# A four-sequence decoder on one core: queries and keys of the attention as two twelve-bit float32r parts in half-array operands, instead of three bf16 parts over the whole array

## The reference, cut to what matters

```python
# WINDOW
scores = jnp.einsum('bnqhd,bnkhd->bnhqk', qp, kp) * scale
attn = jax.nn.softmax(scores, axis=-1)
out = jnp.einsum('bnhqk,bnkhd->bnqhd', attn, vp).reshape(B, L, D)
...
scores = jnp.einsum('bqhd,bkhd->bhqk', q, k) / jnp.sqrt(jnp.asarray(hd, h.dtype))
causal = jnp.tril(jnp.ones((S, S), bool))
scores = jnp.where(causal, scores, jnp.asarray(-1000000000.0, h.dtype))
a = jax.nn.softmax(scores, axis=-1)
out = jnp.einsum('bhqk,bkhd->bqhd', a, v).reshape(B, S, D)
```

## Time and profile before

| what | value |
|---|---|
| three runs | 1493.69, 1497.62 and 1497.46 us; median 1497.46 us |
| profiled execution, span of core 0 | 1493.0 us (the page gives no other time of it) |
| TensorE busy | 1369.8 us, 92% |
| VectorE busy | 1085.1 us, 73% |
| ScalarE busy | 795.1 us, 53% |
| mean DMA rate | 106 GB/s |

### The profile page before, as it was taken

How to read it: one execution, slowest core, us unless ns; L and a number is a source line. 1 busy time by engine, 2 the same in 40 slices (tenths; PEclk the granted TensorE clock), 3 DMA queues, 4 the chain that set the end, 5 groups by cost and what they waited for, 6 DMA issues and landing times. The chain is left out here.

```text
span 1493.0 us, 29555 instructions
## 1 busy us (share of the span) xinstructions
PE 1369.8 (92%) x9483; PEld 763.5 (51%) x9519; DVE 1085.1 (73%) x2623; ACT 795.1 (53%) x1507; POOL 156.6 (10%) x185
## 2 busy tenths in 40 slices
PE   6878989999999999999999999999999989889990
PEld 3556566664454544443353343343545445578990
DVE  5786744457664777789999999998868877563325
ACT  5375755536647666665455465555666545323332
POOL 1101011100100100001010000000000003224223
PEclk8799999999999999999999999999999989999996
DMA  6223323301402542434343333122222231676754
GB/s 230 79 68 102 104 48 86 86 26 27 127 23 80 163 122 52 137 94 121 104 143 98 93 123 86 51 65 53 62 53 56 52 105 57 206 292 194 213 182 179
DMA packets 124482, 158.32 MB, mean 106 GB/s; under 512 B 31372, under 2 KB 103820, under 8 KB 122348
## 3 DMA queue, kind: packets, MB, share of 16 engines
q1 hardware_dynamic: 120930, 147.06, 33.9%
q0 software_dynamic: 3408, 9.38, 1.7%
HBM read 66.38 MB, written 29.44 MB: 64 GB/s over the span
## 5 line engine op out<-in xcount | busy, mean ns | idle before, releaser
L1668 ACT ACTIVATE prob<-ps 128x512 f32<-128x512 f32 (+3 forms) x832 | 404.0, 550 | 202.8 <-PE ps L1441 108.1
L1960 DVE TENSOR_REDUCE mx<-ps 128x1 f32<-128x512 f32 (+3 forms) x512 | 281.3, 585 | 80.3 <-PE ps L1409 42.4
L1441 PE MATMUL ps<-of_expert 99*128 99x512 bf16 (+4 forms) x768 | 252.4, 357 | 8.2 <-DMA of_expert<-mrow 3.3
L1441 PEld LDWEIGHTS ps<-of_expert 99*128 99x128 bf16 (+1 forms) x768 | 73.1, 98 | 95.5 <-ACT prob L1668 35.7
L1476 PE MATMUL ps<-prob,va 128*32 128x512 f32 (+3 forms) x1024 | 117.0, 530 | 0.2
L1407 PE MATMUL ps<-of_expert 120*128 120x512 bf16 x256 | 92.0, 380 | 3.6 <-DVE mx L1960 0.4
L1401 PE MATMUL ps<-of_expert 96*128 96x512 bf16 x256 | 86.7, 381 | 6.2 <-DVE mx L1956 5.3
L1956 DVE CUSTOM_DVE_ANT_0 ps<-ps,room_a 128x512 f32<-128x512 f32 x128 | 86.1, 710 | 5.5 <-PE ps L1401 5.2
L1956 DVE CUSTOM_DVE_ANT_0 ps<-ps,room_b 128x512 f32<-128x512 f32 x128 | 85.9, 708 | 1.7 <-PE ps L1401 1.4
L1398 PE MATMUL ps<-of_expert 96*128 96x128 bf16 (+3 forms) x256 | 72.4, 306 | 9.0 <-DVE mx L1960 7.3
L1658 ACT ACTIVATE mrow<-ps 12x512 bf16<-12x512 bf16 x64 | 37.2, 581 | 77.3 <-PE ps L1423 77.2
(11 more groups left out here) (251 smaller groups left out, 2550.4 us busy)
## 6 DMA issues: line engine op xcount, KB each, us to landing
of_expert<-parts SPq DMA_DIRECT2D x384, 128.0 KB, 2.4
sorted<-zeros SPq DMA_DIRECT2D x27, 650.0 KB, 7.7
room_a<-in_w SPq DMA_DIRECT2D x30, 512.0 KB, 4.1
otc<-oraw SPq DMA_DIRECT2D x256, 32.0 KB, 2.0
room_b<-in_w SPq DMA_DIRECT2D x15, 512.0 KB, 4.2
ct<-in_c SPq DMA_DIRECT2D x8, 512.0 KB, 3.8
of_expert<-in_w SPq DMA_DIRECT2D x8, 512.0 KB, 8.2
wa<-in_attention SPq DMA_DIRECT2D x4, 768.0 KB, 5.0
```

Source lines behind the costliest of these rows:

```text
L1441: i = pe.matmul(dst[:, lo:S], ks[0:rows, h, t], qs[0:rows, h, lo:S], start=(a != MASKED), stop=(a != CAUSAL and not fixed))
L1668: act.activation(prob[:, quad % PROBS, n, lo:S], key_bank(*st)[:, lo:S], ACT.Exp).then_inc(s_exp, 1)
L1960: i = dve.tensor_reduce(mx[:, slot, s, n:n + 1], src[:, 0:width], AX.X, ALU.max)
```

## The change

- A projected query or key is split into two parts instead of three: ACT writes the first as `float32r` (`F32R`), DVE subtracts and writes the second as `float32r`. The step SL is gone, with L1648 and L1933.
- An operand row set of a head is 64 rows instead of 96 to 126: three slots of 16 rows with parts (first by first, first by second, second by first), and a fourth slot for extra rows: two for the maximum, fourteen for the ALiBi lines. Even heads lie in partitions 0 to 63 and odd heads in 64 to 127 (`place_of`), so a score matmul takes up one half of the array's rows. The operands have a tile of their own, `operands`, in float32.
- The scores S and T multiply `float32r` by `float32r`. Corrections, triangles and masks stay bf16 or float16 matmuls over all 128 rows.
- P has two DVE steps instead of four. M transposes 8 columns of float32 instead of 12 of bf16.
- OP issues three DMAs of parts of 256 KB instead of six of 128 KB, and for queries one more that refills the fourth slot from a DRAM scratch (`extra_rows`). At the start a GpSimd DMA casts all extra rows from the input into that scratch, and the keys' extra rows are loaded once, at the end of the first loads.
- The planner's costs follow. TensorE is modelled as two halves (`turn_of_array`): a score matmul waits for its own half, everything else for both. `SWITCH` is added to a correction, triangle or mask. The `LAG` table is another one, so the order of all engines is new.

```diff
+F32R = mybir.dt.float32r
-Q_PARTS = (0, 0, 1, 1, 0, 2)
-K_PARTS = (0, 1, 0, 1, 2, 0)
-ROWS = len(Q_PARTS) * HD
...
+Q_PARTS = (0, 0, 1)
+K_PARTS = (0, 1, 0)
+SLOTS = len(Q_PARTS) + 1
+EXTRA = SLOTS - 1
+HALF = P // 2
...
+def place_of(h):
+
+    return HALF * (h % 2), h // 2
...
-        pe = 0.23
+        pe, after = 0.22, 0.0
+        if a == WINDOW:
+            pe = 0.3
         if a == ALIBI:
-            pe += sum(0.004 + 0.00042 * max(60, hi - lo) for _, lo, hi, _ in corrections(J * g + n, s))
+            after = sum(0.004 + 0.00042 * max(60, hi - lo) for _, lo, hi, _ in corrections(J * g + n, s))
+            after += SWITCH if after else 0.0
         if a == CAUSAL:
-            pe = 0.055 * (s + 2)
+            pe, after = 0.055 * (s + 1), 0.06 + SWITCH
+        pe = (0.0, pe, after, n % 2)
...
+SWITCH = 0.05
...
-LAG = {"IN": -3.7, "CA": 26.5, ("CA", 1): 25.9, "FS": 13.8, "OP": -5.3, ("OP", 0): 1.6, ("OP", 1): -4.0, ("OP", 3): 2.1, "M":
+LAG = {"IN": 12.1, "ZF": -62.0, "EI": 5.1, ("EI", 0): -5.2, ("EI", 1): -6.3, ("EI", 2): 4.6, "CA": -7.7, ("CA", 1): 93.5, ("CA", 2): 103.0, "FS":
...
+def turn_of_array(halves, us, at):
+
+
+    if not isinstance(us, tuple):
+        begin = max(at, *halves)
+        return begin, begin + us, [begin + us] * 2
+    before, main, after, half = us
+    begin = max(at, *halves) if before else max(at, halves[half])
+    halves = [begin + before] * 2 if before else list(halves)
+    end = max(begin + before, halves[half]) + main
+    halves[half] = end
+    if after:
+        end = max(halves) + after
+        halves = [end] * 2
+    return begin, end, halves
...
+            sp.wait_ge(s_extra, 16)
+            sp.dma_start(ks[EXTRA:P:SLOTS, :, :], k_extra).then_inc(s_lines, 16)
...
                     for slot in range(len(slots)):
-                        sp.dma_start(dst[slot:ROWS:len(slots), heads, :], parts[rows, o, slots[slot], g // 2, :]).then_inc(s_op[o][g], 16)
...
+                        sp.dma_start(dst[slot:P:SLOTS, heads, :], parts[:, o, slots[slot], g // 2, :]).then_inc(s_op[o][g], 16)
+                    if o == 0:
+                        alibi = int(kind_of(u) == ALIBI)
+                        if u in (0, NB, 2 * NB):
+                            sp.wait_ge(s_extra, 16)
+                            sp.dma_start(qs[EXTRA:P:SLOTS, heads, :], q_extra[alibi][:, heads, :]).then_inc(s_op[o][g], 16)
+                        else:
+                            sp.dma_start(qs[EXTRA:P:HALF // 2, heads, :], q_extra[0][0:4, heads, :]).then_inc(s_op[o][g], 16)
...
+                    first, pair = place_of(h)
+                    q_, k_ = (z[first:first + HALF, pair, :].bitcast(F32R) for z in (qs, ks))
...
                     elif a == CAUSAL:
-                        pe.matmul(dst[:, 0:(s + 1) * P], qs[0:rows, h, t], ks[0:rows, h, 0:(s + 1) * P], start=True, stop=False)
+                        pe.matmul(dst[:, 0:(s + 1) * P], q_[:, t], k_[:, 0:(s + 1) * P], start=True, stop=False)
                         i = pe.matmul(dst[:, t], identb, tri_q, start=False, stop=True)
...
                         for q in range(NT):
-                            i = pe.transpose(rows_out[0:3 * J, q * P:(q + 1) * P], mp[:, slot, q, :, :].rearrange("p i j -> p (i j)"), identb)
+                            i = pe.transpose(dst[0:2 * J, q * P:(q + 1) * P], mp[:, slot, q, :, :, :].rearrange("p e i j -> p (e i j)"), identf)
...
-                elif kind == "SL":
-                    u, o = st[1:]
-                    act.wait_ge(s_f, nth("QK", u, o, 1))
-                    act.activation(parts[:, o, 1, :, :], rest[:, o, :, :], ACT.Copy).then_inc(s_p1, 1)
...
-                elif kind == "SL":
-                    u, o = st[1:]
-                    dve.wait_ge(s_p1, COUNT[st])
-                    dve.tensor_tensor(parts[:, o, 2, :, :], rest[:, o, :, :], parts[:, o, 1, :, :], ALU.subtract).then_inc(s_p2, 1)
```

More of the change, by code:

```diff
@@ L675, in plan @@
                 continue
-            begin = max([free[found[0][0]]] + [ready[key] for key in found[0][2]]) + lag(strand[heads[i]])
+            begin = max([free[found[0][0]]] + [ready[key] for key in found[0][2]])
+            if found[0][0] == "PE":
+                begin = turn_of_array(halves, found[0][1], begin)[0]
+            begin += lag(strand[heads[i]])
             if best is None or begin < best[0] - 0.02:
@@ L685, in plan @@
         for engine, us, needs, *moved in found:
-            at = max([at, free[engine]] + [ready[key] for key in needs]) + us
+            at = max([at, free[engine]] + [ready[key] for key in needs])
             if engine == "PE":
-                pe_runs.append((len(order), free["PE"], at - us, at))
-            free[engine] = at
+                before = max(halves)
+                begin, at, halves = turn_of_array(halves, us, at)
+                pe_runs.append((len(order), before, begin, at))
+                free[engine] = begin
+            else:
+                at += us
+                free[engine] = at
             at += HOP
@@ L1082, in op_ready @@
             mine = piece_of(u, g)
-            return s_op[o][mine], 16 * len(Q_PARTS) * sum(mine in pieces(v) for v in range(u + 1))
+            return s_op[o][mine], 16 * (len(Q_PARTS) + 1 - o) * (u + 1)
         block = ctx.enter_context(nc.Block())
@@ L1427, in _ @@
                     a, h = kind_of(u), J * g + n
-                    rows = ALL_ROWS if a == ALIBI else ROWS + 3
+                    first, pair = place_of(h)
+                    q_, k_ = (z[first:first + HALF, pair, :].bitcast(F32R) for z in (qs, ks))
                     pe.wait_ge(s_md[g % 2], 16 * (2 * u + g // 2 + 1))
@@ L2277, in constants, with in_parts @@
     bf16 = mybir.dt.np(BF16)
-    def in_parts(v, count=3, dtype=bf16):
+    def in_parts(v, count, dtype):
         out = []
@@ L2288, in constants @@
     line = (slope[:, None] * pos[None, :]).astype(np.float32)
-    one = np.ones((3, H, S), bf16)
     level_from = np.array([LEVEL_FROM[h] for h in range(H)])[:, None]
     tile = np.arange(S)[None, :] // P
-    k_rows, level_rows = [one, np.stack(in_parts(-line))], [one]
+    none, one = np.zeros((H, S), np.float32), np.ones((H, S), np.float32)
+    k_rows, q_rows = in_twelve_bits(-line), [one] * 2
     for s in range(1, NT):
@@ L2295, in constants, with extra @@
         mine = np.broadcast_to((tile == s).astype(np.float32), (H, S))
-        k_rows += [np.stack(in_parts(flat * (np.float32(CLAMP) + line))), np.stack([flat.astype(bf16)] * 3)]
-        level_rows += [np.stack([mine.astype(bf16)] * 3), np.stack(in_parts(-line * mine))]
-    k_rows, level_rows = np.concatenate(k_rows + [one]), np.concatenate(level_rows)
+        k_rows += in_twelve_bits((flat * (np.float32(CLAMP) + line)).astype(np.float32)) + [flat] * 2
+        q_rows += [mine] * 2 + in_twelve_bits((-line * mine).astype(np.float32))
+    def extra(rows, of_max):
+        rows = iter(rows)
+        out = np.stack([of_max if j in MAX_ROW else next(rows) for j in range(HD)])
+        return np.ascontiguousarray(out.reshape(HD, PAIRS, 2, S).transpose(2, 0, 1, 3)).reshape(2 * HD, PAIRS * S)
+    extras = np.concatenate([extra([none] * (HD - 2), none), extra(q_rows, none), extra(k_rows, one)])
     clamp = np.zeros((P, CLAMP_COLS), np.float16)
```

142 lines of the change are left out of this document (65 added, 77 removed), and 25 rows, old and new, of the table LAG.

## The result

The changed kernel takes 1969.51 us (median of 4 runs, 1959.41 to 1985.84) against 1496.15 us for the kernel before (1493.69 to 1497.62, 4 runs): a ratio of 1.318 (95% interval 1.311 to 1.324). I had forecast 1623 us with a range of 1470 to 1700. The direction is right, the size isn't: 473 us slower instead of 126.

The account below looks back on a forecast made before the run. TensorE was taken as the bound in ALIBI, MASKED and CAUSAL. Stage terms of -5, +47, +5 and +79 made 126 us on the 1493.0 us span, 1619, so 1623 us as the runs' median; range 1470 to 1700.

Parts of the forecast that it names:

- the 33 us of losses that ALIBI has: TensorE in ALIBI: 306 us of work end to end in 339; the 33 is added to each TensorE-bound stage.
- the weight load: Float32r scores: load hidden behind 512 columns, but 128-column matmuls take 0.107 us instead of 0.053: WINDOW 27, CAUSAL 7 us.
- The price of a change: TensorE, between 64-row scores and full-array matmuls: about 0.10 us each; WINDOW 8, ALIBI 60, MASKED 50, CAUSAL 97 us.
- The rival of nearly free changes: Every score: changes of shape below about 0.04 us make it faster, 1470 us at 0.025, 1450 at 0; chance 0.27.
- half the price: Rival: a change of shape costs 0.05 us, +16 us in all, 1513 us; chance 0.12.
- a rival at 0.08 us: Each of 1,072 scores entered through a change waits 0.08 us for its weight load: +86, 1709 us; chance 0.10.
- the slack: WINDOW: 188 of 234 us of TensorE work leaves slack, so the stage was forecast at -5 us.
- float32r at half rate: Rival: float32r scores stream at half of bf16's rate, +300 us, over 1900 us; chance 0.03.
- The sum: Stage changes WINDOW -5, ALIBI +47, MASKED +5, CAUSAL +79, experts 0: together 126 us on the span.
- The overlap: Neighbouring scores of different halves run side by side on TensorE, saving at most 23, 20, 37 and 2 us by stage.
- The other edits: SL and two P steps off VectorE, 16 us a stage, counting in MASKED and WINDOW's start; OP, added DMA and order 0.
- What would show it: CAUSAL timeline: score to triangle 0.31 us, triangle to next score 0.16; stages near 229, 386, 380 and 360 us.

Follow-up runs that it names:

- the bf16 run: The kernel before, in bf16 and its old order, with score matmuls taking only the rows from 64 on: 1850.19 us in one run.
- bf16 over all rows: The changed kernel with score matmuls over all 128 rows, reading the upper half of each float32 number as bf16: 1488.87 us, 0.997 of before.
- The run with one half: The changed kernel with every score on rows 0 to 63, odd heads repeating the even heads' scores: 2061.39 us in one run.

## Why the prediction was wrong

**The step that failed** is "Where TensorE is the bound, a stage lasts as long as its work end to end plus the 33 us of losses that ALIBI has": I laid the work out at full clock, since the earlier trace rows had 0.96 to 1.00 in all four stages, and no rival let it fall. The halves themselves make it fall, and that is the larger part of the miss; the smaller is the weight load, below. Out of the mean clock of the stage rows, 174 us of ALIBI, 36 of MASKED and 403 of CAUSAL lie at the half clock (twice what the mean lacks of 1, times the length; 0.18 x 2 x 483 = 174), where before it was 0, 0 and 17. A score with its triangle takes 0.94 us there and 0.59 at full clock, so 0.37 of this time is the clock's: 64, 13 and 149 us, about 226 together. That is an estimate, with the start-to-start times of CAUSAL taken for all stages. The run with triangles four times bears it out for CAUSAL: 485 us less 82 of added work is 403 us at nearly full clock, against 545 - 149 = 396. Shown: the fall comes with 64-row scores in bf16 and in float32r, goes with 128-row ones, and goes when more matmuls over the whole array stand between. Only argued: that what counts is how much of the array is at work.

**The price of a change** was right: 0.10 us each way, by the bf16 run (0.48 against 0.28 for two changes). The Trainium skill's rule that a change of the tiling mode drains TensorE (TensorEngine Tiling (Array Packing), Key Properties) agrees with this trace, where 0.10 us are lost at each change between 64 and 128 rows. The rival of nearly free changes is out, and half the price with it. (That rival's sum has a slip: CAUSAL at 270 + 33 us is 22 over before and not 20.)

**The weight load** was mis-sized. I had let float32's load hide behind 512 columns and put its exposure into a rival at 0.08 us. A visit costs 0.31 us (0.59 less 0.28): 0.20 for the two changes, and 0.11 for float32r; the load is listed 0.09 us longer than bf16's (0.18 against 0.09 to 0.10). The reason that I gave for the rival, that the load begins when the last shape has let go, fits the rows after a change: it begins with the score, at 1272.40. It isn't the whole reason, since over all rows, where no shape changes, 0.08 us stays. Nor does it divide the 0.10 of a change: a bf16 load behind a change also begins with its score (1168.29 in the bf16 halves), so part of the 0.10 may be a load. In WINDOW I had let the slack take up the loads behind 128 columns. It didn't: over all rows WINDOW is 244 us with float32r and 227 with bf16. The rate itself is bf16's: a score of 384 columns is followed by its triangle after 0.37 us (1272.99 to 1273.36) and one of 512 after 0.43, 0.06 us for 128 columns where bf16 has 0.053, so float32r at half rate is out.

**The sum** at full clock, by the same estimate: ALIBI 483 - 64 = 419, MASKED 435, CAUSAL 396, WINDOW 248, the rest 16 us less than before. That is 81, 59, 116, 14 and -16 over before, 254 in all, a span near 1747. I had 47, 5, 79, -5 and 0. With the rival's exposed load I would have come to 1709, some 40 us short of where this kernel would be without the clock. Of the 353 us of span that I missed (1971.8 against 1619), some 226 are the clock's. For the other 127 exposed loads give 118 (1,072 visits times 0.11), but that they come so near is partly luck. By stage they give 33 in ALIBI, where 33 were missed, 28 in MASKED of 55, 56 in CAUSAL where only 36 were missed, and nothing of WINDOW's 19; 16 us less outside the stages even it out. MASKED's other 27 are open, but for the 8 by which it was longer with bf16 over all rows already.

**The overlap** was about right. The run with one half lost 92 us where my upper bound was 82, but part of that is the clock: ALIBI has 245 us at the half clock there instead of 174, MASKED none instead of 36. Taken to full clock by the estimate above, WINDOW, ALIBI, MASKED and CAUSAL lose about 15, 23, 29 and 4 us, some 70 together, against the forecast's 23, 20, 37 and 2.

**The other edits.** M's transposes, OP, P and SL come to -6 us together with the new order (bf16 over all rows against before). So the order adds nothing in sum, as I had taken it; what it does by itself no run shows, and ALIBI was 10 and MASKED 8 us longer.

**What would show it.** Triangle to score: 0.16 as forecast. Scores next to each other start within 0.02 us in 140 of 169 cases in MASKED and 78 of 166 in ALIBI, so the halves work. Score to triangle: 0.43 instead of 0.31. Stages: 248, 483, 448 and 545 us instead of 229, 386, 380 and 360.

The Trainium skill ties the clock to how busy TensorE has lately been and warns of idle gaps (TensorE: Matmul & The Clock Gate, Part 1). By idle gaps alone nothing should have happened here: in CAUSAL TensorE is listed busy for 543.59 of 544.60 us, at a clock of 0.63. The trace doesn't agree with that reading, and the number of rows bears on the clock as well (0.74 with 64 and 0.95 with 128 at the same matmuls).

## What to carry to other kernels

What half-array matmuls gain, they gain where two of different halves stand together. Between full-array matmuls each visit costs 0.20 us at full clock, nearly a 512-column matmul, and float32r adds 0.11. Before taking rows out of a TensorE-bound kernel, ask what clock the emptier array will be granted: here that cost, by the estimate above, as much as all changes of shape together (226 us against 0.20 for each of 1,072 visits, 214). Where the contraction allows it, keep what follows a score in the score's own half: with the triangles there the same result took 1769 us instead of 1970, though that is still slower than the kernel before. A listed busy share of 99% says nothing about changes or clock; the start-to-start times and the clock's row do.

## What the runs showed of the hardware

- With scores over 64 rows or fewer the granted clock of CAUSAL was 0.63 (float32r), 0.73 (bf16) and 0.68 (bf16, 32 or 35 rows), with TensorE listed busy for 99% of it; with scores over 96 rows or more and their triangles it was 0.97 to 0.99. More matmuls over the whole array behind the 64-row scores brought it to 0.97 and made the stage 60 us shorter.
- float32r streams a column in about the time of bf16 (0.06 us for 128), but a float32r score and its triangle over the same 128 rows take 0.08 us more than in bf16 (0.36 against 0.28). Its weight load is listed about twice as long, 191 ns against 97, so that the load is the cause is likely, not shown by itself.
- A change between matmuls over 64 and over 128 rows costs 0.10 us at full clock (0.48 against 0.28 for two). Behind such a change the weight load begins with its matmul (1272.40) and no longer with the matmul ahead of it (1157.63).
- Two 64-row scores of 512 columns in different halves are followed by the next matmul over all rows 0.43 us after the first one's start, in the same half 0.65.
- A half clock doesn't double everything: score and triangle take 0.94 instead of 0.59 us, 1.6 times.
